# Two-block cross attention on one core: every engine's instruction order written anew

## The reference, cut to what matters

```python
# block 0: 16 heads of 64, three layer norms, relative bias, MLP of 1024
qh, kh, vh = ln(x) @ Wq, ln(ctx) @ Wk, ln(ctx) @ Wv
p = softmax((qh @ kh.T + rel_bias[idx]) / 8)
x = x + (p @ vh) @ fc_w.T + fc_b
x = x + gelu(ln2(x) @ W1.T + b1) @ W2.T + b2
# block 1: 16 query heads of 16 over one key/value head, window of 128
p = softmax(where(window, (x @ Wq + bq) @ (ctx @ Wk + bk).T / 4, NEG))
att = (p @ (ctx @ Wv + bv)) @ Wo + bo
g = silu(concat(att, x) @ Wg + bg)
out = att * g + x * (1 - g)
y = rmsnorm(out) * rms_w
return y - mean(y, axis=1)            # over the 128 tokens
```

## Time and profile before

| | us |
|---|---|
| median of 3 runs | 1903.02 (1902.79 to 1907.3) |
| the profiled execution, its own time | 1905.46 |
| its span, first to last instruction | 1903.7 |
| TensorE busy in the span | 1840.5 (97%) |
| VectorE, ScalarE, GpSimd busy | 1518.9 (80%), 1538.4 (81%), 1294.2 (68%) |

### The profile page before, as it was taken

One profiled execution on the slowest core, in us unless ns is written; L12 is line 12 of the kernel. 1 busy time (PEld: TensorE's weight loads), 2 busy tenths in 40 slices (PEclk: granted clock), 3 DMA queues, 4 the chain that ended last, 5 costly groups with the idle time before them and its releaser, 6 DMA issues.

```text
span 1903.7 us, 55010 instructions
## 1 busy us (share of the span) xinstructions
PE 1840.5 (97%) x18660; PEld 1696.0 (89%) x18660; DVE 1518.9 (80%) x6787; ACT 1538.4 (81%) x5586; POOL 1294.2 (68%) x1328
## 2 busy tenths in 40 slices
PE   5999999999999999999999999999999999999974
PEld 4899999999999999999999999999999999999963
DVE  6768888888888888888888888888888888878764
ACT  4688888888888888888888888888888888888864
POOL 3547776767776767777766777766777776777654
PEclk9999999999999999999999999999999999999997
DMA  6434444444444444454434454444444444444332
GB/s 208 131 84 116 111 119 111 115 110 115 107 118 120 115 107 114 104 123 121 116 99 121 101 125 118 114 102 118 111 118 118 110 107 113 112 116 114 88 83 56
DMA packets 215273, 214.49 MB, mean 113 GB/s; under 512 B 29904, under 2 KB 197456, under 8 KB 214992
## 3 DMA queue, kind: packets, MB, share of 16 engines
q1 hardware_dynamic: 214992, 210.97, 44.5%
HBM read 67.23 MB, written 9.44 MB: 40 GB/s over the span
## 4 chain that ended last, share of the span: by engine, by line
PE 94%; DMA 2%; DVE 1%; ACT 1%; POOL 1%; issue 1%; SPq 0%; ACTq 0%; DVEq 0%; POOLq 0%
PE bank L576 12%; PE bank L577 11%; PE bank L578 11%; PE bank L594 8%; PE bank L590 8%; PE bank L591 8%; PE bank L757 7%; PE bank L770 7%; PE bank L582 4%; PE bank L882 4%; PE bank L895 3%; PE bank L583 3%; PE bank L586 3%; PE bank L654 2%; PE bank L600 2%
## 5 line engine op out<-in xcount | busy, mean ns | idle before, releaser
L2574 ACT ACTIVATE soft<-soft,row_min 128x128 f32<-128x128 f32 x1024 | 397.4, 393 | 16.3 <-DVE row_min L1728 16.0
L2494 ACT ACTIVATE soft<-soft,row_min 128x128 f32<-128x128 f32 x1024 | 397.8, 394 | 9.5 <-DVE row_min L1620 9.1
L235 DVE STREAM_TRANSPOSE turned<-soft 128x512 f32<-128x512 f32 x512 | 349.2, 692 | 9.7 <-POOL soft L3032 4.9
L3032 POOL TENSOR_TENSOR soft<-soft,inv_sum 128x512 f32<-128x512 f32 x256 | 267.1, 1044 | 127.3 <-DVE inv_sum L1628 123.3
L3041 POOL TENSOR_TENSOR soft<-soft,inv_sum 128x512 f32<-128x512 f32 x256 | 264.9, 1045 | 93.0 <-DVE inv_sum L1737 93.0
L1620 DVE CUSTOM_DVE_ANT_0 soft<-bank,relb 128x128 f32<-128x128 f32 x1024 | 231.6, 284 | 64.9 <-PE bank L757 64.5
L1728 DVE CUSTOM_DVE_ANT_0 soft<-bank,winb 128x128 f32<-128x128 f32 x1024 | 226.6, 284 | 16.9 <-PE bank L882 14.5
L2494 ACT ACTIVATION_READ_ACCUMULATOR soft<-soft,row_min 128x1 f32 x1024 | 196.7, 192 | 0.0
L2574 ACT ACTIVATION_READ_ACCUMULATOR soft<-soft,row_min 128x1 f32 x1024 | 195.1, 191 | 0.0
L1691 DVE TENSOR_TENSOR hidS<-hid,hidS 128x1024 fp32r<-128x1024 f32 x64 | 120.5, 1883 | 71.5 <-ACT hidS L2545 68.6
L757 PE MATMUL bank<-kT,qT 64*128 64x128 f32 x2048 | 148.7, 285 | 1.5 <-DVE kT L1600 1.4
(11 more groups left out here) (255 smaller groups left out, 6538.3 us busy)
## 6 DMA issues: line engine op xcount, KB each, us to landing
soft<-turned SPq DMA_DIRECT2D x1024, 128.0 KB, 2.8
tokens<-stats_by_row SPq DMA_DIRECT2D x63, 256.0 KB, 3.3
tokens<-in_x SPq DMA_DIRECT2D x32, 256.0 KB, 3.1
raw<-in_x_t SPq DMA_DIRECT2D x32, 256.0 KB, 2.8
x<-in_x SPq DMA_DIRECT2D x32, 256.0 KB, 3.1
out<-gate SPq DMA_DIRECT2D x63, 128.0 KB, 3.1
tokens<-in_ctx SPq DMA_DIRECT2D x31, 256.0 KB, 2.8
raw<-in_ctx_t SPq DMA_DIRECT2D x31, 256.0 KB, 2.8
```

The lines of the kernel that those rows point to most:

```text
L235: return eng.transpose(turned[:, slot, :, s % 2, :, :].rearrange("p j h b -> p h j b"), soft[:, s, :, :].rearrange("p h (j a) -> p h j a", ...
L2494: last = act.activation(soft[:, s, h, :], soft[:, s, h, :], ACT.Exp, bias=row_min[:, s, h:h + 1], scale=-1.0, accum_out=row_sum[:, s, h:h ...
L2574: last = act.activation(soft[:, s, h, :], soft[:, s, h, :], ACT.Exp, bias=row_min[:, s, h:h + 1], scale=-1.0, accum_out=row_sum[:, s, h:h ...
L3032: pool.tensor_tensor(soft[:, m % NS0, :, :], soft[:, m % NS0, :, :], inv_sum[:, m % NS0, :].unsqueeze(2).broadcast_to([P, QUAD, SEQ]), ALU ...
```

## The change

All five lists are written anew: 1054 lines stand for 1056. The functions are the same, each step is issued as often as before with the same operands in SBUF, and only the order of the calls differs, with the PSUM banks and the drains that TensorE waits for. The lists come from a scheduler outside the kernel, which now counts more time for VectorE and GpSimd operations that read and write SBUF alone. The first ring has three banks instead of four in the loop, and bank 0 is used by itself:

```diff
-        ring0 = banks[0:4]
+        ring1 = banks[1:4]
         ring4 = banks[4:8]
```

TensorE's loop, at its head and at its end:

```diff
             for r in range(3, NG - 3):
-                scores(r, 0, (ring0[r % 4], ring4[r % 4]), (("v_out", 4 * r),), (("min1", 8 * r - 13),))
-                fc_lo(r - 1, 2, ring0[(r + 2) % 4])
+                scores(r, 0, (banks[0], ring4[r % 4]), (("v_out", 4 * r),), (("min1", 8 * r - 12),))
+                fc(r - 1, 2, ring1[(r + 1) % 3])
...
-                kv_k(r, ring4[(r + 2) % 4], ("q_out", 4 * r + 2))
...
-                fc(r, 2, ring0[(r + 3) % 4])
-                pv(r, 3, ring0[r % 4], ("min1", 8 * r - 6))
+                kv_k(r + 1, ring4[r % 4], ("min1", 8 * r - 6))
+                pv(r, 3, ring4[(r + 2) % 4], ("min1", 8 * r - 5))
```

and the place of `center_out(r - 2, 0)` in it, which now stands behind the hi part of `mlp_out(r - 1, 1, ...)`:

```diff
+                mlp_out(r - 1, 1, 0, ring1[r % 3])
+                mlp_out(r - 1, 1, 1, ring1[r % 3])
+                center_out(r - 2, 0, ring1[(r + 1) % 3], ("min0", 8 * r + 7))
-                center_out(r - 2, 0, ring4[(r + 3) % 4], ("min0", 8 * r + 7))
-                mlp_out(r - 1, 1, 0, ring4[r % 4])
-                mlp_out(r - 1, 1, 1, ring4[r % 4])
```

More of the change, by code:

```diff
@@ new lines, in tensor_program @@
+            fc(1, 3, banks[3])
+            proj_v(2, 0, banks[2], ("q_out", 10))
+            fc_lo(1, 3, banks[3])
+            proj_k(2, 2, banks[4], ("min0", 18))
+            pv1(0, 0, 0, banks[0], ("o_lo", 8))
+            pv1(0, 0, 1, banks[0])
+            scores1(0, 1, (banks[2], banks[6], banks[3], banks[7]), (("v_out", 9),), (("min0", 20),), (("x1", 2),),
+                (("min0", 19),))
+            proj_q(2, 2, banks[4], ("k_out", 11))
+            out_mm(0, 0, banks[2], ("min1", 5))
@@ new lines, in tensor_program @@
+            pv(2, 2, banks[6], ("hid_out", 8))
+            fc_lo(2, 0, banks[2])
+            proj_v(2, 3, banks[4], ("min0", 23))
+            pv1(0, 1, 0, banks[3], ("v_out", 11))
+            pv1(0, 1, 1, banks[3])
+            center_out(0, 0, banks[0], ("min0", 24))
+            mlp_out_lo(1, 1, 0, banks[1])
+            mlp_out_lo(1, 1, 1, banks[1])
+            out_mm(0, 1, banks[0], ("y_out", 1))
+            turn_x2(1, banks[3], ("o1_lo", 2))
+            fc(2, 1, banks[2])
+            proj_q1(1, banks[1], ("x2", 2))
@@ new lines, in tensor_program @@
+            fc_lo(NG - 4, 2, banks[1])
+            scores(NG - 3, 1, (banks[0], banks[5]), (("min0", 233),), (("min0", 234),))
+            proj_v(NG - 3, 0, banks[2], ("k_out", 118))
+            fc(NG - 4, 3, banks[1])
+            proj_q(NG - 3, 2, banks[3], ("q_out", 118))
+            fc_lo(NG - 4, 3, banks[1])
+            proj_k(NG - 3, 2, banks[6], ("o_lo", 116))
+            pv1(NG - 5, 0, 0, banks[2], ("v_out", 117))
+            pv1(NG - 5, 0, 1, banks[2])
+            center_out(NG - 6, 1, banks[0], ("min0", 235))
@@ new lines, in tensor_program @@
+            pv1(NG - 5, 1, 1, banks[0])
+            center_out(NG - 5, 0, banks[5], ("min0", 239))
+            mlp_out(NG - 4, 1, 1, banks[1])
+            mlp_out_lo(NG - 4, 1, 0, banks[1])
+            mlp_out_lo(NG - 4, 1, 1, banks[1])
+            out_mm(NG - 5, 1, banks[3], ("v_out", 119))
+            turn_x2(NG - 4, banks[6], ("min0", 240))
+            proj_q_lo(NG - 2, banks[2])
+            out_mm_lo(NG - 5, 1, banks[3])
+            proj_q1(NG - 4, banks[0], ("o1_lo", 56))
+            proj_q1_lo(NG - 4, banks[0])
@@ new lines, in tensor_program @@
+            proj_v(NG - 1, 0, banks[1], ("o_lo", 123))
+            scores(NG - 1, 1, (banks[7], banks[5]), (("min0", 249),), (("min0", 250),))
+            fc_lo(NG - 2, 2, banks[4])
+            fc(NG - 2, 3, banks[4])
+            proj_q(NG - 1, 2, banks[3], ("q_out", 126))
+            fc_lo(NG - 2, 3, banks[4])
+            proj_k(NG - 1, 2, banks[0], ("k_out", 126))
+            pv1(NG - 3, 0, 0, banks[1], ("v_out", 125))
+            pv1(NG - 3, 0, 1, banks[1])
+            center_out(NG - 4, 1, banks[7], ("min0", 251))
@@ new lines, in tensor_program @@
+            scores(NG - 1, 3, (banks[6], banks[2]), (("o_lo", 125),), (("kv_turn", 31),))
+            mlp_out(NG - 2, 0, 1, banks[4])
+            mlp_out_lo(NG - 2, 0, 0, banks[4])
+            mlp_out_lo(NG - 2, 0, 1, banks[4])
+            proj_v(NG - 1, 2, banks[5], ("q_out", 128))
+            pv1(NG - 3, 1, 0, banks[0], ("hid_out", 123))
+            pv1(NG - 3, 1, 1, banks[0])
+            center_out(NG - 3, 0, banks[6], ("min0", 255))
+            mlp_out(NG - 2, 1, 0, banks[4])
+            mlp_out(NG - 2, 1, 1, banks[4])
```

2082 lines of the change are left out of this document (1009 added, 1073 removed).

## The result

The changed kernel takes 1908.03 us (median of 12 runs, 1906.36 to 1910.12) beside 1903.08 of the kernel before (12 runs). The ratio is 1.0020, with a 95% interval of 1.0012 to 1.0029: slower by 0.2%. A second comparison on another occasion gives 1908.94 to 1903.87, ratio 1.0028 (1.0018 to 1.0038). So some 5 us are lost in the medians, where the prediction had 0.3 gained. It had given no time above 1908.0 to its own four terms: the measured medians lie just above that.

A forecast was written before the change was run, and what follows sets the result against it. TensorE's own instructions were taken to bound the kernel; start -1.5, kv_k +1.3, shape changes +1.4, loop waits 0 and end -1.5 sum to -0.3, so 1902.7 us from a median of 1903.02, range 1896 to 1911.

The forecast's parts named there:

- its own four terms: Start, kv_k and shape changes, loop waits, end: with rival 3 between 1899.3 and 1908.0 us, chance 0.63.
- rival 2: Loop: GpSimd's x_hat_lo comes late for center_out (L934), then out_mm; 0.3 a round, 7.8 us, about 1910.5; chance 0.20.
- kv_k in 26 rounds: Loop, TensorE: kv_k ahead of pv costs 0.92 in place of 0.87, +0.05 a round, +1.3 us.
- the signs that the prediction named: Forecast wrong if the period differs from 56.72 by over 0.2 or both ends' idle time changes by over 5 us.
- The start: Up to pv(0, 0): -1.5 us, from 1.2 of earlier statistics and 0.3 of filled waits; bounds -2.2 to +1.6.
- 1.2 us of earlier statistics: Start: var_c ahead of wk's lo parts ends VectorE's 0.81 wait and more; 0.8 to 1.6 reach the first scores.
- 0.3 of waits of VectorE on the norms are filled: Start, between scores and spread: the lo part of w2's first half fills VectorE's waits, gaining 0.3 us.
- The upper bound, +1.6: Start, worst case: 1.3 us of SyncE's issues for q1_gx_in and 1.1 of VectorE, less 0.8.
- The loop: 26 rounds: +1.3 us from kv_k's new place, no new waits, a period of 56.77.
- The shape changes: TensorE at both ends: 13 more changes of tile shape at about 0.11 each, +1.4 us at most, taken as +1.4.
- The end: Last 104 us: -1.5 us, from kv_k(NG - 1) -0.85 and the fourth norm1 -0.65; upper bound +0.7.
- Both of its places: End: kv_k(NG - 1) in the 1.03 hole ahead of pv(NG - 1, 3), -0.85; fourth norm1 no longer behind times_gate, -0.65.

The follow-up runs named there:

- changed again: The changed kernel, unchanged, run again as a control on one chip with the kernel before: ratio 1.0028 to it, +5.07 us in the median.
- e4: Changed kernel with the loop's kv_k(r + 1) moved between full tiles, fc_lo(r, 1) and proj_k_lo(r + 1): ratio 1.0034 to the kernel before, +7.79 us.
- e6: Changed kernel with GpSimd's norm1(NG - 1, 0, 3) put back behind times_gate(NG - 2, 1) at the end: +4.76 us against the kernel before.
- before again: The kernel before, unchanged, run again as a control on one chip with the changed kernel: median 1903.87 us.
- e1: Changed kernel with all five lists of groups 0 to 2 from the kernel before, banks renumbered: ratio 1.0005 to the kernel before, +1.11 us.
- e8: Kernel before with kv_k(NG - 1) moved ahead of pv(NG - 1, 3), where TensorE waits 1.03 us: ratio 1.0001, -0.13 us.
- e5: Changed kernel with w2's lo part moved behind turn0(0, 1) and q1_gx_in behind spread0(0, 0): ratio 1.0023 to the kernel before, +4.19 us.
- e7: Changed kernel with e5's edits and three VectorE start steps moved (min1(1, 0, 3), x1_sum(1), turn1(0, 1, 3)): ratio 1.0009 to the kernel before, +1.48 us.
- e2: Changed kernel with scores(3, 0) in the first loop round waiting for the 11th min1, not the 12th: +3.13 us against the kernel before.
- e9: Kernel before with VectorE's min1(1, 0, 3) moved behind inv1(1, 0, 0), k_out(3, 0), stats_x(4) and turn1(1, 0, 0): ratio 1.0024, +4.16 us.

## Why the prediction was wrong

The forecast had 0.3 us gained and 5 were lost. That the range held the time was luck: its upper end came from rival 2, a wait in the loop that didn't happen. The step that failed is the first one, where the stretches were chosen: windows were read for the first 60 us, the loop and the last 104, the start was priced up to pv(0, 0), and the sum went on with "kv_k in 26 rounds". Groups 0 to 2 between the first pv and the loop had no term. They hold most of the loss: by the stages 3.5 us (means of 133.4 over changed, changed again, e4 and e6, and of 129.9 over before, before again, e1 and e8). That TensorE was never idle there before (0.84 us in 180) was a reason to look, not to pass over: a stretch without idle time has none to give back, and any late handing-over adds some. Nor would the signs that the prediction named have shown the error: they watched the period (56.76 for 56.72) and the idle time of the two ends (23.3 and 23.4 in the first 60 us, 35.9 and 31.8 in the last 104), and neither passed its bound.

**The start** was forecast at -1.5 and came out at +1.4 (means 23.1 and 21.7, same traces). It was the sum of two gains, and neither came. The 1.2 us of earlier statistics should have reached the first scores; scores(0, 0) stands at 33.5 on average in the eight traces with the changed start and at 32.8 in the five with that of before, 0.7 later. SyncE's rows show where the gain went. They are its writing of ctx's statistics (L356) and its reading of them back (L371) in the profile after:

```profile
17.56 0.55 SPq L356 DMA_DIRECT2D stats_by_row<-first_rows  x1
...
20.74 0.33 SPq L371 DMA_DIRECT2D x<-stats_by_row  x1
```

In the kernel before they stand at 18.05 and 20.27. The write is issued 0.5 sooner, but SyncE then waits 1.6 us for it to land and not 0.6 (1.5 and 0.4 in the second pair of traces). Why it lands later is open; no run tests it. The other gain, "0.3 of waits of VectorE on the norms are filled", is the second faulty link: scores to first spread takes 10.43 us in both orders, as said at e5. From the issue of the spread to pv(0, 0) it is 0.5 more on average (6.0 and 5.5), in e5 and e7 too, so the two loads ahead of it don't make it. The upper bound, +1.6, is close by luck: it was 1.3 of issues, which cost nothing, and 1.1 on VectorE less 0.8.

**The loop** was forecast at +1.3 with no wait, and that is what it did: 1362.1 and 1363.2 us for 24 rounds (means of before, before again and e8; of changed, changed again, e1 and e6), 0.04 a round. But the step behind the +1.3 doesn't hold. kv_k takes 0.95 to 0.96 to pv's start in the rounds of the profile after, not 1.02; less the 0.10 that pv pays anyway this is 0.86, the same as the 0.87 of its old place, and by the prediction's own way of counting the term would be nothing. So that the number fits is luck. That kv_k's place carries a price, a tenth for the place tried, is shown by e4; that it makes these 0.04 is not, since its old place among proj_k steps was not tried in the new loop.

**Rival 2** was worked out well and didn't happen. On GpSimd, TensorE and ScalarE, one round of the profile after:

```profile
958.92 1.28 POOL L3109 TENSOR_TENSOR x<-x,rows 128x512 f32<-128x512 f32 x1
960.16 1.49 POOL L3085 TENSOR_TENSOR xT<-raw,xT 128x512 fp32r<-128x512 f32 x1
961.75 1.61 POOL L3017 TENSOR_TENSOR stat<-stat,half_exp 128x2 f32<-128x2 f32 x1
963.33 0.74 POOL L3144 TENSOR_TENSOR o1T<-ag,o1T 128x256 fp32r<-128x256 f32 x1
...
964.54 0.27 PE L934 MATMUL bank<-o1T,center 128*128 128x256 f32 x1
...
964.90 0.37 ACT L2585 CAST o1T<-bank 128x256 fp32r<-128x256 f32 x1 [0.48 <-PE bank L934]
...
965.59 0.39 PE L590 MATMUL bank<-wog,o1T 128*128 128x512 f32 x1
```

x_hat_lo ends at 964.07, 0.47 ahead of L934 (0.5 was forecast for x1_b2 at 1.30), and o1_hi ends 0.32 ahead of out_mm. x1_b2 does take 1.28, and it is now rstd_c (L3017) that takes 1.61.

**The shape changes** (+1.4) were never seen apart. In the second stage 3.0 of the 3.5 us are idle time, so at most some 0.5 is left for them there. In the traces nine or ten of the additional ones stand in the last 300 us.

**The end** was forecast at -1.5 and gave some -0.3 by the stages (300.85 over the four traces with the end of before, 300.58 over the nine with the changed one), less than the spread of the traces. Both of its places were tried alone, and neither gives anything (e6, e8): each was taken at the full length of an instruction or hole, without asking what the next waiting step waits for. The idle time did fall, by 2.4 us from scores(28, 0) to the last matmul (four traces of before's end against eight of the changed one), but TensorE's own time rose by 2.1. Taken from windows of half a microsecond as busy time times the missing part of the granted clock, an estimate, about 1 of that is matmuls at the lower clock; the ten changes of shape at 0.11 would make the rest. No run parts the two.

With what was measured the sum is +1.4 + 3.5 + 1.1 - 0.3 = 5.7, beside +4.95 and +5.07 in the medians; the traces don't fix it closer than that.

## What to carry to other kernels

When all orders change at once, go through the program in stretches that leave none out, and price first those in which the bounding engine has no idle time today: a handing-over that gets late there can reach the end whole (1.59 us of wait in e2, 1.9 back) or more than whole (e9). A loop in which nothing waits doesn't mean that its first round won't, since its waits are written for the steady state and meet a start that is laid out otherwise. A hole on the bounding engine is worth its length only if the step behind it sets what comes next, and idle time that goes is no gain if the engine's own work gets longer beside it, as at the end here.

## What the runs showed of the hardware

Contention between VectorE and GpSimd in SBUF was moved, not removed. Groups of instructions between 300 and 1600 us (count, busy us and mean ns behind it), of before and then of after:

```profile
L1691 DVE TENSOR_TENSOR hidS<-hid,hidS 128x1024 fp32r<-128x1024 f32 x46 | 92.4, 2008 | 49.8 <-ACT hidS L2545 49.8
L1784 DVE SCALAR_TENSOR_TENSOR ag<-ag,rrms,rows 128x256 f32<-128x256 f32 x46 | 28.7, 624 | 0.0
L3111 POOL TENSOR_TENSOR x<-x,rows 128x512 f32<-128x512 f32 x23 | 52.4, 2276 | 0.0
L3019 POOL TENSOR_TENSOR stat<-stat,half_exp 128x2 f32<-128x2 f32 x23 | 19.8, 862 | 6.4 <-DVE stat L1519 6.4
```

```profile
L1689 DVE TENSOR_TENSOR hidS<-hid,hidS 128x1024 fp32r<-128x1024 f32 x46 | 58.2, 1266 | 14.5 <-ACT hidS L2543 14.5
L1782 DVE SCALAR_TENSOR_TENSOR ag<-ag,rrms,rows 128x256 f32<-128x256 f32 x46 | 52.6, 1144 | 0.0
L3109 POOL TENSOR_TENSOR x<-x,rows 128x512 f32<-128x512 f32 x23 | 29.4, 1277 | 0.0
L3017 POOL TENSOR_TENSOR stat<-stat,half_exp 128x2 f32<-128x2 f32 x23 | 36.9, 1606 | 2.4
```

hid_lo (L1691, L1689) and x1_b2 (L3111, L3109) get shorter by 0.74 and 1.00 us each time; x_hat (L1784, L1782) and rstd_c, a step of 128x2 elements (L3019, L3017), get longer by 0.52 and 0.74. The pairs have changed. Before, x1_b2 started beside hid_lo and rstd_c beside x_hat; now, in all 23 rounds, x_hat starts 0.17 behind x1_b2 and rstd_c 0.17 behind hid_lo. In the round shown above, on VectorE:

```profile
959.10 1.39 DVE L1782 SCALAR_TENSOR_TENSOR ag<-ag,rrms,rows 128x256 f32<-128x256 f32 x1
...
961.59 1.21 DVE L1689 TENSOR_TENSOR hidS<-hid,hidS 128x1024 fp32r<-128x1024 f32 x1
```

The one that starts first keeps its plain length, 1.28 for x1_b2 and 1.21 for hid_lo, and the second ends after it. rstd_c takes 1.61 behind hid_lo, and GpSimd's other step of this shape (L3009) 0.70. That even 256 elements can be held up so long fits the lock of the Trainium skill ("SBUF — State Buffer", the section on SBUF's two separate sides), under which the one that comes second waits for the first's whole instruction. VectorE is busy 15.6 us less over the loop and GpSimd 5.0, and since TensorE sets the loop, none of it is in the time.

The clock was not expected to enter at all. A wait of 2.04 us in the midst of dense matmuls cost 3.5: the wait, and 1.5 at half clock behind it (e9, one execution). The wait of 1.59 at the same place of the changed kernel, and one of 1.74 in e4, left the clock as it was.

TensorE's pace also varies at the start. Behind the first L582 matmuls of 256 columns start 0.21 apart, as they do in e9 at half clock, and later 0.12; the windows of the profile have 1.00 for the granted clock there all the same. In the trace of before 15 starts in a row stand at 0.21, in before again 6, which makes 0.8 of the 1.6 us between their first stages.
